# Attention stage rebuilt: spikes by ACT's sign, sums of value tiles two apart, one-hots in 16-bit pairs, down weights awaited expert by expert

## What is computed

```python
Q = lif(layer_norm(xn @ Wq.T + bq, gq, betaq), 1.0)     # 0 or 1; K and V alike
attn = Dh - (q_sum + k_sum.T - 2 * Q @ K.T) + log_pe_bias(N, N)
out = lif((attn * scale) @ V, 0.5)                      # 16 heads of 16, 0 or 1
s = lif(layer_norm(out @ Wo.T + bo, go, betao), 1.0)
ids = argmin(dist2(rms_norm(xn), centroids))            # one of 8 experts a row
ffn = (a * silu(g)) @ down_w[ids] + xn                  # a, g = split(rms_norm(xn) @ up_w[ids])
return x + s * silu(ffn)
```

## Time and profile before

| | |
|---|---|
| median of 3 runs | 384.81 us (384.73 to 385.58) |
| the profiled execution | 387.33 us, its span 385.5 us |
| busy over the span | PE 95%, DVE 82%, ACT 58%, POOL 59% |
| DMA | 45.44 MB, mean 118 GB/s |
| granted TensorE clock | 0.99 of full speed |

### The profile page before, as it was taken

How to read it: one execution, slowest core, us unless ns; L and a number is a source line. 1 busy time by engine, 2 the same in 40 slices (tenths; PEclk the granted TensorE clock), 3 DMA queues, 4 the chain that set the end, 5 groups by cost and what they waited for, 6 DMA issues and landing times.

```text
span 385.5 us, 9398 instructions
## 1 busy us (share of the span) xinstructions
PE 365.9 (95%) x2583; PEld 309.6 (80%) x2584; DVE 314.4 (82%) x785; ACT 224.9 (58%) x611; POOL 225.8 (59%) x296
## 2 busy tenths in 40 slices
PE   8999999999999999977699999999999999999992
PEld 4888888888877888865588888888888888888881
DVE  6789999998668999997477788887777777787884
ACT  4598788888743343451555555555555655555561
POOL 4677777787601225664456666666666666666643
PEclk9999999999999999999899999999999999999997
DMA  6686768463299121439122222223223222332000
GB/s 221 214 280 199 212 172 280 144 195 114 84 189 237 56 82 29 137 110 298 55 68 75 83 66 73 86 86 95 64 81 94 74 81 86 92 95 63 28 17 0
DMA packets 31874, 45.44 MB, mean 118 GB/s; under 512 B 4113, under 2 KB 25810, under 8 KB 31716
## 3 DMA queue, kind: packets, MB, share of 16 engines
q1 hardware_dynamic: 25200, 29.73, 26.8%
q0 software_dynamic: 6416, 15.26, 13.5%
q10 hardware_dynamic: 228, 0.10, 0.1%
HBM read 36.84 MB, written 15.63 MB: 136 GB/s over the span
## 4 chain that ended last, share of the span: by engine, by line
PE 66%; DVE 16%; DMA 6%; issue 5%; ACT 3%; SPq 1%; POOL 1%; ACTq 0%; DVEq 0%; POOLq 0%
PE bank L646 20%; PE bank L454 16%; PE bank L665 12%; DMA row_a<-rows_a,slot_id 4%; PE bank L629 3%; DVE up_lo L1209 3%; DMA down_sb<-in_down_w 2%; DVE s_out L1201 2%; PE bank L618 2%; DVE a_sp L1113 2%; PE bank L433 2%; ACT d_hi L848 2%; PE bank L519 2%; PE bank L386 1%; PE bank L364 1%
## 5 line engine op out<-in xcount | busy, mean ns | idle before, releaser
L1268 DVE TENSOR_TENSOR d_lo<-down_sb,d_hi 128x1024 fp32r<-128x1024 f32 x38 | 46.6, 1225 | 35.2 <-ACT d_hi L848 35.2
L848 ACT ACTIVATE d_hi<-down_sb 128x1024 fp32r x38 | 40.3, 1060 | 47.8 <-issue 22.6
L1416 POOL DMA_INDIRECT row_a<-rows_a,slot_id x39 | 40.5, 1037 | 45.1 <-DVE e_o L1282 25.4
L1450 POOL DMA_INDIRECT out_x<-e_o,slot_id x39 | 44.8, 1149 | 19.4 <-issue 14.4
L646 PE MATMUL bank<-up_hi,e_xh 128*128 x156 | 52.0, 415 | 0.0
L1422 POOL DMA_INDIRECT row_s<-rows_s,slot_id x39 | 39.5, 1013 | 19.4 <-issue 11.6
L646 PE MATMUL bank<-up_hi,e_xl 128*128 x156 | 48.5, 392 | 1.0 <-DVE e_xl L1220 1.0
L646 PE MATMUL bank<-up_lo,e_xh 128*128 x156 | 48.5, 392 | 0.0
L822 ACT ACTIVATE e_xh<-bank 128x256 fp32r<-128x256 f32 x39 | 15.0, 385 | 39.8 <-issue 16.0
L768 ACT ACTIVATE junk<-bank 128x256 bf16<-128x256 f32 x96 | 35.4, 379 | 4.6 <-PE bank L454 4.3
L646 PEld LDWEIGHTS bank<-up_hi,e_xl 128*128 128x128 f32 x156 | 29.2, 188 | 7.9 <-DVE e_xl L1220 1.5
(11 more groups left out here) (227 smaller groups left out, 985.3 us busy)
## 6 DMA issues: line engine op xcount, KB each, us to landing
up_raw<-in_up_w SPq DMA_DIRECT2D x16, 512.0 KB, 4.1
rows_a<-xn SPq DMA_DIRECT2D x32, 129.0 KB, 2.4
rows_a<-in_x SPq DMA_DIRECT2D x8, 512.0 KB, 13.0
down_sb<-in_down_w SPq DMA_DIRECT2D x8, 512.0 KB, 6.2
xs<-in_x SPq DMA_DIRECT2D x7, 512.0 KB, 4.0
rows_s<-s_out SPq DMA_DIRECT2D x8, 256.0 KB, 2.9
blk_tab<-in_blocks SPq DMA_DIRECT2D x1, 1024.0 KB, 5.2
row_a<-rows_a,slot_id POOLq DMA_INDIRECT x39
```

The source lines that it names most:

```text
L848: act.activation(d_hi[:, :, :], down_sb[:, bass.ds(e, 1), :, :].rearrange("p a c n -> p (a c) n"), ACT.Copy).then_inc(d_high, 1)
L1268: V.tensor_tensor(d_lo[:, :, :], down_sb[:, bass.ds(e, 1), :, :].rearrange("p a c n -> p (a c) n"), (d_hi if k < ST else d_end)[:, :, :].b ...
L1416: G.indirect_dma_start(row_a[s % 4][:, :], None, rows_a, bass.IndirectOffsetOnAxis(ap=slot_id[:, s:s + 1], axis=0), bounds_check=N - 1, oo ...
L1450: G.indirect_dma_start(out, bass.IndirectOffsetOnAxis(ap=slot_id[:, s:s + 1], axis=0), e_o[s % 4][:, :], None, bounds_check=N - 1, oob_is_ ...
```

## The change

- Spikes of attention (`a_sp`) are made by ACT with `Sign`, so they are -1 or 1. `wo_hi` and `wo_lo` are halved, and half the column sums of the weights, made by eight one-column matmuls at tile 3 (`half_sums`), are added to the output bias. The sign's bias is a half-integer that DVE computes from `thr2` (`step_n`, signal `step_set`), so that no argument is 0.
- DVE adds value tiles j and j + 2 (`pairs`, 30 sums, bf16): 16 in the last steps of the projection loop, 8 and 6 during attention. In `attend_near` the tiles 2 and 4 away on a side become one matmul with the sum; at the ends of the sequence single tiles stay.
- The one-hots are laid out with two row tiles next to each other innermost, all operands in bf16 (tables `col_two`, `slot_tile`, `base16`, made by POOL's iota; one iota more).
- `cvec_done` is made between the two halves of `attend_near(1)`.
- The down loads go out at other chunks, two of them in halves, each with a semaphore of its own expert (`down_put`). SP passes them on in order as `down_ready`. ACT waits for expert e's for slots 0 to 2 and for all from slot 3 on. Each chunk's put of spikes comes one chunk later in SP's list, and the last three loads behind all puts.
- The order of ACT's and of DVE's work in stage 3 is rewritten; the last expert's `high_parts` moves into the loop over the chunks.

```diff
-DOWN_FREED = {1: (4,), 3: (5,), 5: (0, 6), 7: (1, 2, 3, 7)}
+DOWN_FREED = {5: ((0, 0, 2), (6, 0, 2)), 6: ((4, 0, 2), (1, 0, 1), (2, 0, 1)),
+              7: ((1, 1, 2), (2, 1, 2)), 8: ((3, 0, 2), (5, 0, 2), (7, 0, 2))}
...
+NP = NT - 2
+P_FIRST, P_THEN = 16, 8
...
+        pair_a, _ = place("pair_a", [P, P_FIRST, D], BF16, at=at_set)
+        pair_b, _ = place("pair_b", [P, 2 * P_THEN, D], BF16, at=at_down + 2 * NT * D)
...
+        def pair_of(j):
+            return pair_a[:, j, :] if j < P_FIRST else pair_b[:, j - P_FIRST, :]
...
-            for c in range(NCH + 1):
-                if c in DOWN_FREED:
-                    sp.wait_ge(at_done, DC * (c + 1))
-                    for e in DOWN_FREED[c]:
-                        sp.dma_start(down_sb[:, e, :, :], down_w[e].rearrange("(c p) n -> p c n", p=P)) \
-                            .then_inc(down_loaded, 16)
-                if c:
-                    sp.wait_ge(s_made, CH * c)
-                    sp.dma_start(rows_s[(c - 1) * CT:c * CT, :].rearrange("(t p) n -> p t n", p=P),
-                                 s_out[(c - 1) % 2][:, :, :]).then_inc(s_put[(c - 1) % 2], 16)
+            def load_down(c):
+                sp.wait_ge(at_done, DC * min(c + 1, NCH))
+                for e, h0, h1 in DOWN_FREED.get(c, ()):
+                    part = slice(h0 * HC // 2, h1 * HC // 2)
+                    sp.dma_start(down_sb[:, e, part, :], down_w[e].rearrange("(c p) n -> p c n", p=P)[:, part, :]) \
+                        .then_inc(down_put[e], 16)
...
+            def put_spikes(c):
+                sp.wait_ge(s_made, CH * (c + 1))
+                sp.dma_start(rows_s[c * CT:(c + 1) * CT, :].rearrange("(t p) n -> p t n", p=P),
+                             s_out[c % 2][:, :, :]).then_inc(s_put[c % 2], 16)
...
+            def down_landed(e):
+                halves = sum(1 for loads in DOWN_FREED.values() for d, _, _ in loads if d == e)
+                sp.wait_ge(down_put[e], 16 * halves)
+                sp.sem_inc(down_ready, 1)
+            for c in range(NCH - 1):
+                load_down(c)
+                if c > 1:
+                    put_spikes(c - 2)
+            load_down(NCH - 1)
+            put_spikes(NCH - 3)
+            down_landed(0)
+            put_spikes(NCH - 2)
+            put_spikes(NCH - 1)
+            load_down(NCH)
+            for e in range(1, E):
+                down_landed(e)
...
+                if k == 3:
+                    pe.wait_ge(w_split, 4)
+                    for n in range(DC):
+                        for c in range(DC):
+                            for m, w in enumerate((wo_hi, wo_lo)):
+                                last = pe.matmul(xt_bank[:, D + n:D + n + 1], w[:, c, n * P:(n + 1) * P].bitcast(F32),
+                                                 ones32[:, 0:1], start=(c == 0 and m == 0), stop=(c == 1 and m == 1))
                 last.then_inc(xt_done, 1)
...
-                inside = [(b, side, j) for b in range(CH) for d in (2, 4, 8, 16)
-                          for side, j in ((0, CH * c + b - d), (1, CH * c + b + d)) if 0 <= j < NT]
-                for n, (b, side, j) in enumerate(inside):
-                    pe.matmul(ps[:, b * P:(b + 1) * P], v_sp[:, j, hs], tri[:, side, :],
-                              start=(n == 0), stop=False)
+                after(pe, paired, min(CH * c + 6, NP))
+                inside = []
+                for b in range(CH * c, CH * c + CH):
+                    for side, way in enumerate((-1, 1)):
+                        far = b + 4 * way
+                        if 0 <= far < NT:
+                            inside.append((b, side, pair_of(min(far, far - 2 * way))))
+                        elif 0 <= b + 2 * way < NT:
+                            inside.append((b, side, v_sp[:, b + 2 * way, :]))
+                        inside += [(b, side, v_sp[:, b + d * way, :]) for d in (8, 16) if 0 <= b + d * way < NT]
+                for n, (b, side, source) in enumerate(inside):
+                    at = (b - CH * c) * P
+                    pe.matmul(ps[:, at:at + P], source[:, hs], tri[:, side, :], start=(n == 0), stop=False)
...
-            for h in range(DC):
-                attend_near(1, h)
+            attend_near(1, 0)
...
             pe.wait_ge(neg_made, 1)
             for c in range(DC):
...
             last.then_inc(cvec_done, 1)
+            attend_near(1, 1)
             pe.wait_ge(ld_b, 16)
...
-                    last = pe.matmul(bank[6][:, 0:2 * ST], low_hot[q][:, n, :],
-                                     high_id[q][:, n, :, :].rearrange("p a s -> p (a s)"),
+                    last = pe.matmul(bank[6][:, 0:2 * ST], low_hot[q][:, n // 2, :, n % 2],
+                                     high_id[q][:, n // 2, :, :, n % 2].rearrange("p a s -> p (a s)"),
                                      start=(q == 0 and n == 0), stop=(q == 1 and n == HT - 1))
...
-                               scale=1.0 if p < 3 else -1.0).then_inc(w_high, 1)
+                               scale=1.0 if p < 3 else -0.5).then_inc(w_high, 1)
...
-            def high_parts(e):
-                for half in range(DC):
+            def high_parts(e, halves=range(DC)):
+                for half in halves:
                     if e == E - 1:
...
+                    if e == E - 2 and half == 0:
+                        act.wait_ge(at_done, DC * 5)
                     act.activation(up_hi[:, e, half, :], up_raw[:, e, half, :], ACT.Copy,
                                    scale=vc[:, FS_ + half:FS_ + half + 1]).then_inc(up_high, 1)
...
-            for c in range(NCH - 1):
-                squares_out(c % 2, c // 2)
-                if c == 3:
+            def attention_spikes(c):
+                s = c % 2
+                after(act, wo_done, 2 * (c - 1))
+                for h in range(DC):
+                    act.wait_ge(at_done, DC * c + h + 1)
+                    act.activation(a_sp[s][:, h, :], at_bank(c, h)[:, :], ACT.Sign, bias=step_n[:, 0, h:h + 1],
+                                   scale=way).then_inc(at_spiked, 1)
+            act.wait_ge(step_set, 1)
+            attention_spikes(0)
+            for c in range(1, NCH):
+                attention_spikes(c)
+                if c == NCH - 1:
+                    high_parts(E - 1, (1,))
+                squares_out((c - 1) % 2, (c - 1) // 2)
+                if c == 4:
                     act.wait_ge(pos_done, 2)
-                if c < NCH - 3:
-                    high_parts(c + 2)
+                if c < E - 2:
+                    high_parts(c + 1)
+                elif c == E - 2:
+                    high_parts(E - 1, (0,))
             def turned_high(k, i):
...
-            high_parts(E - 1)
...
-                        act.wait_ge(down_loaded, 16 * E)
+                    if k < 4:
+                        act.wait_ge(down_ready, e + 1)
+                    elif k == 4:
+                        act.wait_ge(down_ready, E)
...
+                if k == 3:
+                    V.tensor_copy(half_sums, xt_bank[:, D:D + DC]).then_inc(sums_kept, 1)
...
-                elif part in (5, 7, 9):
-                    at = 4 * (part - 5)
+                elif part == 5:
+                    dve.wait_ge(sums_kept, 1)
+                    made = V.tensor_tensor(bc[:, 6:8], bc[:, 6:8], half_sums, ALU.add)
+                elif part in (6, 8, 10):
...
+                    made = V.tensor_scalar(way, scale, 0.0, 2.0, ALU.is_ge, ALU.mult)
+                elif part == 12:
+                    made = V.tensor_scalar(way, way, -1.0, None, ALU.add)
+                elif part == 13:
+                    made = V.tensor_tensor(size, scale, way, ALU.mult)
+                elif part == 14:
+                    made = V.tensor_scalar(size_inv, size, 1e-30, None, ALU.max)
+                elif part == 15:
+                    made = V.reciprocal(size_inv, size_inv)
...
+            def pairs(first, until):
+                for j in range(first, until):
+                    V.tensor_tensor(pair_of(j), v_sp[:, j, :], v_sp[:, j + 2, :], ALU.add).then_inc(paired, 1)
...
-                if 0 <= k - 9 < 10:
+                if 0 <= k - 9 < 16:
...
+                if 0 <= k - 17 < P_FIRST:
+                    dve.wait_ge(spiked, 3 * (k - 17 + 3))
+                    pairs(k - 17, k - 16)
...
-            def attention_spikes(c, halves=range(DC)):
-                s = c % 2
-                after(dve, wo_done, 2 * (c - 1))
-                for h in halves:
-                    dve.wait_ge(at_done, DC * c + h + 1)
-                    V.tensor_scalar(a_sp[s][:, h, :], at_bank(c, h)[:, :], scale, thr2[:, h:h + 1], ALU.mult,
-                                    ALU.is_ge).then_inc(at_spiked, 1)
...
+            dve.wait_ge(bias_n, 16)
             dve.wait_ge(cvec_done, 1)
             step(V.tensor_scalar(thr2[:, :], bank[7][:, 0:DC], scale, 0.5, ALU.mult, ALU.mult))
             step(V.tensor_scalar(thr2[:, :], thr2[:, :], 0.5, None, ALU.add))
```

(43 more changed lines are left out.)

46 lines of the change are left out of this document (27 added, 19 removed).

## The result

The changed kernel takes 382.04 us (median of 7 runs, 380.67 to 383.14) against 385.31 us of the kernel before in the same session (384.63 to 387.45): ratio 0.991, interval 0.9883 to 0.9937. A second series gave 382.54 against 385.91, ratio 0.9911 (0.988 to 0.9942). It is faster, by some 3.3 us, where 10.8 were forecast (374.0 us) and the range ended at 381.0. The profiled execution took 383.09 us with a span of 381.3, 4.2 less than the span of before.

A forecast was written before the change was run, and what follows sets the result against it. PE's issue was taken as the bound, then DVE's backlog, then one down-weight load; -12.5 us up to slot 2 (attention's gain included), +0.9 and +0.8 in the projection loop gave -10.8: 374.0 us, range 370.5 to 381.

The forecast's parts named there:

- part 6: Projection loop: column sums at tile 3 cost 0.9 us, pair sums and extra output-bias steps 0.8 us.
- the put in part 5: Between attention and expert slots: the put of the last spikes into DRAM takes 2.9 us.
- Where PE is bound: Attention: PE issues without gaps, so 88 fewer small matmuls in chunks 2 to 7 save 4.9 us.
- the threshold chain: Before the first spikes: DVE's tiny operations for the half-integer threshold cost 0.5 us, bounds 0 and 1.5.
- Rival 1: Attention's tail: DVE stays the bound, pairs and one-hots miss double rate, last spikes 3 us later; 377 us, chance 0.14.
- Rivals 3 and 4: Attention: ACT's queue order becomes the clock, 381 us, chance 0.06; or sign and squares switch tables, 378 to 422, chance 0.04.
- Part 6a: Projection loop, tile 3: eight one-column fp32 matmuls on PE cost 0.9 us (0.2 to 1.1).
- Part 6b: Projection loop: 16 pair sums and 6 more `output_bias` steps on busy DVE cost 0.8 us (0 to 3).
- rival 2: Projection loop: pair sums ahead of `keep_qt` in DVE's queue cost 0.3 us on nine tiles; 377 us, chance 0.12.
- the growth of 0.1: Projection loop: its cycle of 2.69 us growing over 0.1 would show the prediction wrong.
- Part 5, the transition: From attention to slot 2's `e_h`: 14.3 us earlier, less 0.3 for a gather and 1.5 for load contention, 12.5 gained.
- The expert loop is untouched: Expert loop from slot 3 on: no change in time.

The follow-up runs named there:

- loads_late: The changed kernel with SP issuing the last three down loads only after slot 1's spike rows have landed; 383.8 us.
- loads_early: The changed kernel with the last three down loads issued with chunk 7's loads, ahead of the last puts; median 383.45 us.
- no_sums: The changed kernel without the eight one-column matmuls at tile 3, so the output bias is wrong; 382.1 us.
- sums_f32r: The changed kernel with the eight column-sum matmuls in one pass on fp32r operands with two columns; 380.79 us.
- the repeat: The changed kernel run once more without any edit; 382.54 us, ratio 0.9911 to the kernel before.
- own_last: The changed kernel with DVE making `e_o` of slots 0 and 1 behind `e_h` of slot 3; 385.67 us.
- free_rows: own_last, with DVE copying residual columns so the row buffers of slots 0 and 1 are freed without the spikes; 381.62 us.
- free_f32r: free_rows with the eight column-sum matmuls in one pass on fp32r operands with two columns; 379.16 us.
- gathers_first: free_f32r with POOL issuing row gathers, from slot 6 on, ahead of spike gathers and scatters; 380.58 us.

## Why the prediction came out wrong, step by step

Three steps failed, and the paragraphs below take them in the forecast's order: the prices of the loop's new work (part 6), the put in part 5, and the expert loop, which got no term at all.

**Where PE is bound (right).** Attention is bound by what PE issues: 4.89 us came off, where the forecast had 4.6 (4.9 for 88 matmuls and 0.2, less 0.5 for the threshold). The other ends agree too: the threshold chain ran to 120.47 with the first sign at 120.6 and cost PE 0.41 us (forecast 0.5), a sign takes 0.777 us (0.7 to 0.8), and the 2.15 and 1.04 us gaps of DVE are gone. Rival 1 is out, and the low one-hot fell from 2282 to 1216 ns, `high_id` from 813 to 486 (one line's instructions):

```profile
L1282 DVE TENSOR_TENSOR low_hot<-col_two,low x2: 1216/1216/1216, 135.8 to 141.4; 128x2048 bf16<-128x2048 bf16 x2
```

So the trace agrees with section 5.1 of the Trainium skill's "Vector Engine (DVE) Microarchitecture Reference": two-byte operands with step one innermost pass two elements a cycle, and here the rate rose 1.9 and 1.7 times (the old low one-hot also had a four-byte operand, the old `high_id` only the broadcast innermost). The pair sums, 0.284 us for 256, lie nearer the bound from above (0.33) than the 0.2 taken.

**Rivals 3 and 4 (out).** PE waited for `a_sp` once, 0.41 us. There is one ACT_TABLE_LOAD in the trace, at 2.91 us as before, so sign shares the loaded table; no run shows a switch.

**Part 6a, the column sums (0.9; measured 1.8, net 1.1).** The misread row is the earlier trace rows: its `x4` are records, and each fp32 matmul leaves two. Two matmuls, not four, lay between 17.0 and 17.3. The bound from above, 1.1, was made of the same reading.

**Part 6b, the pair sums in the loop (0.8; measured 1.7 to 2.2 from tile 14 to 31).** Within the bounds of 0 to 3, and below rival 2's 2.7. The cycle went from 2.72 us a tile to 2.82 and 2.85, at the growth of 0.1 that the prediction had named as a sign of being wrong. 1.0 to 1.6 us of the loss are the sums, by two experiments; 0.5 to 0.6 remain, and which of the other edits in the loop has them wasn't tried.

**Part 5, the transition (7.9 of the 12.5; measured 5.8 to 6.3 up to `turn_hidden(2)`).** The mechanism was right, as was the time of the last spikes: 8.0 us behind the end of `turn_rows(0)` by forecast, 8.3 in the trace (168.78 to 177.04). The gather took 5.0 to 5.5 us, forecast 3.5 + 1.5, so contention had about its size. What failed is the put: 2.9 us, against 4.7 from the last `s_out` to POOL's gather. The 2.9 of the earlier trace rows is the page's median of eight puts, and the trace of before had the single ones: the first three took 2.3 us each, the last two, issued at 178.37 and 180.93 beside the down loads, took 6.8 and 5.0 (the issues of a window around each: count, KB, us to landing):

```profile
rows_s<-s_out SPq DMA_DIRECT2D x1, 256.0 KB, 6.8
...
rows_s<-s_out SPq DMA_DIRECT2D x1, 256.0 KB, 5.0
```

In the changed kernel the last put landed after 3.85 us, some 1 us more than was taken. The other 0.83 us lie between its landing and POOL's gather; they are the same in all ten profiles in which such a landing is recorded and this gather is what it releases, that of before too, and the forecast has no term for them. Without the late loads the put took 3.95 us to landing, so they are not what makes it slower than 2.9. What is stays open: POOL's gather of slot 3's rows starts 0.77 us ahead of this put in the changed kernel and in loads_late, and 2.1 us ahead in loads_early, the one profile with 3.2 us, and no run moves it alone. The sum also has a slip: 172.0 + 2.9 + 3.5 is 178.4, not 178.7, which hid 0.3 of the miss.

**"The expert loop is untouched" (failed).** Slots 2 to 5 give back 1.5 to 1.9 us. The 3.68 us gap of before had the clock's fall behind it (0.64 and 0.51 of full speed from 186 to 190 us), ahead of `turn_hidden(2)`. The forecast compared the two times of `e_h(2)`, and so let that loss go with the gap. The new gap of 3.21 us brings it back, now behind `turn_hidden(2)` (0.59 and 0.55 from 188 to 192 us). PE alone, before and then changed:

```profile
186.00:188.00 2.00, 1.24 (x5) 0.64 0.00 0
188.00:190.00 2.00, 2.00 (x10) 0.51 0.10 33
```

```profile
188.00:190.00 2.00, 1.64 (x6) 0.59 0.00 0
190.00:192.00 2.00, 2.00 (x6) 0.55 0.39 101
```

Over the four us the clock is short of full speed by 1.7 us in both, which is the size of what slots 2 to 5 give back. A shorter gap may not: ahead of `turn_hidden(2)` or `turn_rows(4)` idle times of 1.93 to 2.60 us had the clock at 1.00 behind them (loads_late, no_sums, loads_early, sums_f32r), all those of 3.21 to 5.79 had it near 0.5.

**The sum.** Forecast: +0.9 and +0.8 in the loop, -4.6 attention, -7.9 transition, 0 behind it: -10.8. Profiled: -0.4 ahead of tile 1, +3.0 to tile 14, +2.2 to tile 31, -4.9, -6.3, +1.5 to `turn_hidden(5)` and +0.6 to the end: -4.2 with rounding. The 6.6 us between the two are -0.4 from the start, 2.1 to tile 14 (1.85 of them the clock fall that the repeat hasn't), 1.4 for the loop's pairs, -0.3 in attention, 1.6 in the transition and 2.1 behind it, with rounding. Part of the last is idle time at `turn_rows(38)`, 0.71 us in the changed kernel and none before. The median missed by more, 8.0 us (382.04 against 374.0): the forecast took it to lie 2.5 us below the profiled execution, as in its three runs of before, and in the changed kernel that is 1.05.

**The deeper miss** is what stands behind the last put. The prediction followed the chain to `e_h(2)` and stopped. It goes on through `o_done` and the four row buffers to `turn_rows(4)`, and through POOL's queue to slot 6. loads_late, loads_early and own_last each shorten one place and pay at the next; own_last pays all. With the chain cut (free_rows) it is 381.62 us, and with the sums in one pass besides (free_f32r) the same work takes 379.16 us, 6.7 below the kernel before of its series. That the cut alone brought less than the 3.5 to 5 us expected of it is not explained to the end: slot 6's gap took 2.58 us of it, the clock an amount that differs between executions.

## What to carry to other kernels

Behind a shortened wait follow the chain past the instruction that it releases, through the ring buffers and queues that this one frees, until it meets work that is late anyway; what is not cut there only moves. Take a price from instructions in the same place, not from a median over all places (2.9 us for eight puts of 2.3 to 6.8), add what lies between a landing and the start of what waits for it, and count records against the code before dividing by them. Where the clock falls behind a gap, count that loss as a row of its own, since a shorter gap can bring it back in full.

## What the runs showed of the hardware

- An fp32 matmul of one column costs 0.21 us (1.71 us for eight), in two records; in one pass with two columns 0.11 us (0.90 for eight).
- The granted clock fell to about half in two of the profiles behind the column sums at 24 us (0.53 and 0.61) and not in others of the same kernel or the same instructions. In own_last it was at 0.50 from 190 to 192 us while PE did nothing. In gathers_first it fell behind two idle times of 0.60 and 1.20 us with one turning between them, and behind one of 2.58 us in free_rows, while the same 2.58 us in free_f32r left it at 1.00. What decides there, these runs don't tell.
- A put of 256 KB from the last producer's end to the start of POOL's gather that waits for it took 4.6 to 4.9 us beside 1.5 MB of loads and 4.8 without them, and 3.2 us in one profile; 0.83 us of it lie between its landing and the gather, in all ten profiles that record the landing. A gather of 128 rows took 2.9 and 3.6 us without those loads and 4.1 to 5.5 beside them.
- POOL issues an indirect DMA every 1.31 us at best. A slot needs three, 3.9 us of a slot's 5.05, so by estimate a backlog is worked off at 1.1 us a slot.
- Mean clocks of whole executions differ within one kernel: 0.987 to 0.998 in loads_early, whose quickest execution (380.39 us) is the one at 0.998, and 0.982 to 0.997 in free_f32r, whose slowest (382.47 us) is the one at 0.982. In between the times don't follow this mean strictly (loads_early: 384.43 us at 0.993, 381.62 at 0.989).
- In two of fourteen profiles one release of ACT and DVE by a matmul came 3.3 and 3.4 us behind its recorded end, where some 0.1 us is usual. What held it isn't in the traces.
